# Dense stage of a three-stage transformer block: gates worked out behind the first weight split, norms of four tiles inside the last unit, odd residuals added on VectorE

## The reference, cut to what matters

```
x = rmsnorm(src + sa, norm1_w);  flat = x.reshape(S, C)
shared = swiglu(flat @ W_shared_in) @ W_shared_out
g_probs = softmax(flat @ Wg_gate + group_bias);  g_idx = argmax(g_probs)
e_probs = softmax(where(in_group, flat @ We_gate + expert_bias, -inf))
p_expert = e_probs * g_prob;  topv, topi = top_k(p_expert, 2);  w = scatter of topv
h = swiglu(flat @ W1_shared);  routed = sum over 8 experts of (h @ W2_experts[e]) * w[:, e]
out = rmsnorm(x + shared + routed, norm2_w)          # and the caller adds: x2 + out
```

## Time and profile before

| | |
|---|---|
| runs shown | 3588.77 us median of 3 (3583.67 to 3590.61) |
| profiled execution | 3591.36 us |
| its span, first to last instruction | 3589.5 us |
| TensorE busy | 3316.7 us, 92% of the span |
| VectorE / ScalarE / GpSimd busy | 1851.6 / 1485.4 / 1631.7 us |
| mean granted TensorE clock | 0.964 of full speed |

### The profile page before, as it was taken

The page is one execution under the profiler, slowest core; times in us unless marked ns, Lnnn a source line. Parts: engine busy times, 40 slices in busy tenths (PEclk is TensorE's granted clock), DMA queues, the critical chain, the costliest instruction groups (busy, mean ns, idle before and its releaser), DMA issues. The chain is left out here.

```text
span 3589.5 us, 52832 instructions
## 1 busy us (share of the span) xinstructions
PE 3316.7 (92%) x19140; PEld 2847.9 (79%) x19140; DVE 1851.6 (52%) x3010; ACT 1485.4 (41%) x2749; POOL 1631.7 (45%) x1122
## 2 busy tenths in 40 slices
PE   5999999999999999999999988899999586799995
PEld 4888888888888888888888876777777465578995
DVE  4454555555455555555545557566566537432213
ACT  3455555555555555555555541244344214221000
POOL 4354555555455555545545543143144035146663
PEclk9999999999999999999999989899999798899998
DMA  5211111111111011111111004100000300123220
GB/s 194 76 33 36 45 45 44 35 35 46 36 45 46 24 45 46 43 38 45 33 36 45 27 15 139 55 1 26 3 1 1 108 16 1 49 74 118 83 83 24
DMA packets 116510, 170.33 MB, mean 47 GB/s; under 512 B 12288, under 2 KB 89472, under 8 KB 107520
## 3 DMA queue, kind: packets, MB, share of 16 engines
q1 hardware_dynamic: 113408, 158.23, 14.0%
q0 software_dynamic: 2816, 8.46, 0.7%
HBM read 143.52 MB, written 23.13 MB: 46 GB/s over the span
## 5 line engine op out<-in xcount | busy, mean ns | idle before, releaser
L427 POOL TENSOR_TENSOR es<-es,e 128x512 f32<-128x512 f32 x480 | 622.7, 1297 | 966.7 <-ACT e L493 966.5
L489 ACT ACTIVATE e_hl<-sc 128x512 fp32r<-128x512 f32 x512 | 325.2, 635 | 739.1 <-DVE sc L557 738.8
L585 PE MATMUL ps_p<-c_hi,wkv_lo 128*128 128x512 f32 x1024 | 402.4, 393 | 4.5 <-PEq L115 4.5
L515 DVE TENSOR_TENSOR k_lo<-ps_p,k_hi 128x512 fp32r<-128x512 f32 x256 | 175.9, 687 | 438.9 <-ACT k_hi L455 438.9
L585 PE MATMUL ps_p<-c_lo,wkv_hi 128*128 128x512 f32 x1024 | 401.9, 393 | 0.0
L585 PE MATMUL ps_p<-wkv_lo,c_hi 128*128 128x512 f32 x1024 | 401.6, 392 | 0.0
L585 PE MATMUL ps_p<-wkv_hi,c_lo 128*128 128x512 f32 x1024 | 401.5, 392 | 0.0
L585 PE MATMUL ps_p<-c_hi,wkv_hi 128*128 128x512 f32 x1024 | 398.8, 389 | 0.0
L515 DVE TENSOR_TENSOR v_hl<-ps_p,v_hl 128x512 fp32r<-128x512 f32 x256 | 177.2, 692 | 428.8 <-ACT v_hl L455 427.9
L585 PE MATMUL ps_p<-wkv_hi,c_hi 128*128 128x512 f32 x1024 | 398.3, 389 | 0.0
L557 DVE TENSOR_SCALAR sc<-ps_s,topi 128x512 f32<-128x512 f32 x512 | 380.0, 742 | 0.3 <-PE ps_s L635 0.2
(11 more groups left out here) (399 smaller groups left out, 7136.4 us busy)
## 6 DMA issues: line engine op xcount, KB each, us to landing
raw<-in_ctx_t SPq DMA_DIRECT2D x64, 1024.0 KB, 4.9
dense_raw<-in_L_ffn_W_experts SPq DMA_DIRECT2D x64, 256.0 KB, 3.0
raw<-in_L_xattn_Wkv SPq DMA_DIRECT2D x4, 1024.0 KB, 5.0
q_hi_scratch<-qa_qh SPq DMA_DIRECT2D x16, 256.0 KB, 2.5
q_lo_scratch<-qa_ql SPq DMA_DIRECT2D x16, 256.0 KB, 3.4
q_hi<-q_hi_scratch SPq DMA_DIRECT2D x32, 128.0 KB, 5.1
q_lo<-q_lo_scratch SPq DMA_DIRECT2D x32, 128.0 KB, 4.7
o_t_scratch<-o_sb SPq DMA_DIRECT2D x32, 128.0 KB, 2.3
```

The costliest lines, as they stand in the source:

```text
L427: g.tensor_tensor(ES[:, GL], ES[:, GL], e, ALU.add).then_inc(summed, 1)
L489: a.activation(E2[:, s % 2, :, 0, :], sc, ACT.Exp, scale=DH ** -0.5).then_inc(exp_hi, 1)
L515: v.tensor_tensor(kv_slice(False, kind, n), ps_view(u, kind), kv_slice(True, kind, n).bitcast(F32), ALU.subtract).then_inc(p_free, 1)
L585: mm = t.matmul(ps_p[:, par % 2, :], lhs, rhs, start=m == 0, stop=m == 3 * KC - 1)
```

## The change

Three edits, all in or around the dense stage.

1. `route` moves from the end of stage_ffn_attend into stage_dense, behind VectorE's four splits of the first weights and ahead of its first multiplication. LG now lives outside both stages, in place of SEL, and SEL, which the dense stage now allocates itself, takes LG's part as a buffer of that stage. The comparison that sets SEL signals `chosen`, for which `rank` on TensorE waits. The exponential stands on ScalarE behind its four weight casts and ahead of the first silu. The scratch tiles RK and G lie in HS instead of PT, and the constant EARLIER comes as 16 more columns of ORDER instead of by a transfer of its own in the stage before. The instructions of `route` are the same.
2. In the last unit, VectorE takes the moments of tiles 0 to 3 and then finishes them (`finish(0)`: the small instructions, the scaling) right after the addition of slot B, ahead of the additions of slots 4 to 7. Each of tiles 4 to 7 has its moments taken right after its own last addition. Then comes `finish(1)`.
3. In `finish`, VectorE adds the residual of the odd tiles itself, after scaling; GpSimd adds that of the even ones. GpSimd still writes all eight tiles, in order.

```diff
 stage_ffn_attend, at its end on VectorE:
             v.wait_ge(logits_read, 1)
-            route(v, link)
 and on ScalarE:
-            a.wait_ge(g_shifted, 1)
-            a.activation(G[:, 14:20, :], G[:, 4:10, :], ACT.Exp).then_inc(g_expd, 1)

 stage_dense, GpSimd:
             for j in range(B):
-                g.wait_ge(scaled, j + 1)
-                g.tensor_tensor(OUT[:, j], ROWS[:, j], X2[:, j], ALU.add).then_inc(final, 1)
-                g.wait_ge(final, j + 1)
+                if j % 2:
+                    g.wait_ge(odd_final, j // 2 + 1)
+                else:
+                    g.wait_ge(scaled, j + 1)
+                    g.tensor_tensor(OUT[:, j], ROWS[:, j], X2[:, j], ALU.add).then_inc(final, 1)
+                    g.wait_ge(final, j // 2 + 1)
                 g.indirect_dma_start(out.rearrange("b p f -> (b p) f"), ...

 stage_dense, ScalarE:
                 a.copy(W_hi[:, A_, q], RAW[:, q]).then_inc(w_hi_done, 1)
+            a.wait_ge(g_shifted, 1)
+            a.activation(G[:, 14:20, :], G[:, 4:10, :], ACT.Exp).then_inc(g_expd, 1)
             branch(0)

 stage_dense, VectorE:
             v.wait_ge(order_in, 16)
+            route()
             v.tensor_copy(META[:, :, E_ALL], TOKEN).then_inc(meta_set, 1)
...
+            def moments_of(j):
+                moments(v, c, mom[:, j], ROWS[:, j], stats[:], rs[:, 3, 0:1])
+
+            def finish(hb):
+                s_ = slice(hb * H_, (hb + 1) * H_)
+                link(v.tensor_tensor(rs[:, 0], mom[:, s_, 0], mom[:, s_, 0], ALU.mult))
+                link(v.tensor_tensor(rs[:, 0], rs[:, 0], mom[:, s_, 1], ALU.add))
+                link(v.tensor_scalar(rs[:, 0], rs[:, 0], RMS_EPS, None, ALU.add))
+                rsqrt_cols(v, c, rs[:, 1], rs[:, 0], rs[:, 2])
+                for j in range(hb * H_, (hb + 1) * H_):
+                    v.scalar_tensor_tensor(out=ROWS[:, j], in0=ROWS[:, j], scalar=rs[:, 1, j % H_:j % H_ + 1], in1=N2[:], op0=ALU.mult, op1=ALU.mult
+                                           ).then_inc(scaled, 1)
+                    if j % 2:
+                        v.wait_ge(x2_in, 16 * B)
+                        v.wait_ge(scaled, j + 1)
+                        v.tensor_tensor(ROWS[:, j], ROWS[:, j], X2[:, j], ALU.add).then_inc(odd_final, 1)
             for u, (p, o) in enumerate(UNITS):
+                last = u == len(UNITS) - 1
...
+                    if last and j >= H_:
+                        v.wait_ge(added, B + m + 1)
+                        for jj in (range(H_) if j == B else (j,)):
+                            moments_of(jj)
+                    if last and j == B:
+                        finish(0)
+            finish(1)
-            v.wait_ge(added, B + NS * len(UNITS))
-            for hb in range(2):
-                ... the moments, the small instructions and the scaling of four tiles, twice

 stage_dense, TensorE, in rank():
+                t_.wait_ge(chosen, 1)
                 t_.matmul(bank(4)[:, 0:B], BEFORE, SEL[:, 0, :], start=True, stop=False, skip_group_check=True)

 program, outside both stages:
-        SEL = sb("sel", [P, 1, B])
+        LG = sb("lg", [P, GROUPS_E + E_ALL, B])
```

More of the change, by code:

```diff
@@ L1417, in _ @@
             sp.dma_start(WV[:], wv).then_inc(wkv_in, 16)
-            pieces = ((I[:], ident), (ROPE_T[:], rope_t), (EARLIER[:], earlier.partition_broadcast(P)),
+            pieces = ((I[:], ident), (ROPE_T[:], rope_t),
                       (BIAS[:, 0:GROUPS_E], g_bias.partition_broadcast(P)), (BIAS[:, GROUPS_E:], e_bias.partition_broadcast(P)),
@@ L1718, in hidden_piece, with stage_dense @@
     return [(dst[:, s], rows[:, :, s * HID + j * P:s * HID + (j + 1) * P]) for s in range(2)]
[L1721 removed]
+def stage_dense(nc, x2_d, xs_d, bs_d, ms_d, wts, order, norm2, ROWS, XT_hi, XT_lo, META, LG, RAW, out):
     w_in, w_out, w1, w2 = wts
@@ L1743, in stage_dense @@
         ONES = sb("ones", [P, P])
-        ORDER = sb("order", [P, 2 * P + B + B + 1])
+        ORDER = sb("order", [P, 2 * P + B + B + 1 + EPG * EPG])
         BEFORE, TOKEN, EDGE, I = (ORDER[:, a:b] for a, b in ((0, P), (P, P + B), (P + B, P + 2 * B + 1), (P + 2 * B + 1, 2 * P + 2 * B + 1)))
+        EARLIER = ORDER[:, 2 * P + 2 * B + 1:].rearrange("p (i j) -> p i j", i=EPG)
+        SEL = sb("sel", [P, 1, B])
+        RK = flat(HS[:])[:, 0:2 * EPG * EPG * B].rearrange("p (a i j b) -> p a i j b", a=2, i=EPG, j=EPG)
+        G = flat(HS[:])[:, 2 * EPG * EPG * B:][:, 0:30 * B].rearrange("p (n b) -> p n b", b=B)
         N0 = sb("n0", [P, 1])
@@ L2111, in _, with program @@
             g.sem_clear(range(nums[0], nums[-1] + 1))
-def program(nc, x, ctx_t, mask, ident, rope, causal, rope_t, earlier, order, wq, wkv, front, attend, w_proj, ffn, dense, norm2, out):
+def program(nc, x, ctx_t, mask, ident, rope, causal, rope_t, order, wq, wkv, front, attend, w_proj, ffn, dense, norm2, out):
     scratch = lambda n, s: nc.dram_tensor(n, s, F32, kind="Internal").ap()
@@ L2152, in program @@
         first_pieces = [piece for q in range(GP) for piece in hidden_piece(dense[0], DENSE_RAW, q, q)]
-        stage_ffn_attend(nc, ffn, (ident, rope_t, earlier), ROWS, XT_hi, XT_lo, META, SEL, first_pieces)
-        stage_dense(nc, x2, xs, bs, ms, dense, order, norm2, ROWS, XT_hi, XT_lo, META, SEL, DENSE_RAW, out)
+        stage_ffn_attend(nc, ffn, (ident, rope_t), ROWS, XT_hi, XT_lo, LG, first_pieces)
+        stage_dense(nc, x2, xs, bs, ms, dense, order, norm2, ROWS, XT_hi, XT_lo, META, LG, DENSE_RAW, out)
 FRONT = ["L0_xattn_Wo", "L0_xattn_bo"] + ["L0_attn_" + n for n in ("w_cq", "g_qnorm", "w_ckv", "g_kvnorm", "w_krope", "w_gate")]
@@ L2175, in tables @@
     order = np.concatenate([np.triu(np.ones((P, P)), 1), np.arange(TOK).reshape(B, P).T,
-                            np.tile(np.arange(B + 1) * P, (P, 1)), np.eye(P)], 1)
-    return {"order": f(order), "ident": f(np.eye(P)), "rope": f(rope), "causal": f(causal), "rope_t": f(rope_t), "earlier": f(np.tril(np.ones((EPG, EPG)), -1))}
+                            np.tile(np.arange(B + 1) * P, (P, 1)), np.eye(P), np.tile(np.tril(np.ones((EPG, EPG)), -1).reshape(1, -1), (P, 1))], 1)
+    return {"order": f(order), "ident": f(np.eye(P)), "rope": f(rope), "causal": f(causal), "rope_t": f(rope_t)}
 def kernel(**inputs):
@@ L2196 @@
     out = nc.dram_tensor("out", (B, P, D), F32, kind="ExternalOutput").ap()
-    program(nc, *(ap[n] for n in ("x", "ctx_t", "mask", "ident", "rope", "causal", "rope_t", "earlier", "order", "L0_xattn_Wq", "L0_xattn_Wkv")),
+    program(nc, *(ap[n] for n in ("x", "ctx_t", "mask", "ident", "rope", "causal", "rope_t", "order", "L0_xattn_Wq", "L0_xattn_Wkv")),
             [ap[n] for n in FRONT], [ap[n] for n in ATTEND], ap["L0_attn_w_proj"], [ap[n] for n in FFN], [ap[n] for n in DENSE], ap["L0_ffn_norm2_w"], out)
```

60 lines of the change are left out of this document (40 added, 20 removed).

## The result

The changed kernel took 3572.19 us (median of 6 runs, 3564.33 to 3572.79) beside 3589.55 us for the kernel before (6 runs, 3583.67 to 3592.53). The ratio is 0.9949, 95% interval 0.9936 to 0.9962: 18.3 us of 3589.55, between 14 and 23. A second timing gave 0.9947 (0.9933 to 0.9960). The forecast was 3570.0 in 3563 to 3578, a gain of 18.8 us.

A forecast was written before the change was run, and what follows sets the result against it. The prediction took a chain of waits through the dense stage and tail as the bound, mostly TensorE's; 6.1 + 12.7 = 18.8 us off 3591.36 gave 3572.6, and 2.6 less for the median 3570.0, range 3563 to 3578.

The forecast's parts named there:

- Part 1, route: At the dense stage's border: route's 6.07 us get covered, 4.2 us to spare at the third chunk; 6.1 us gained.
- The clock: TensorE's clock at the border: no difference taken, with bounds of 1.4 us less and 2.8 us more.
- Rival (c): At the border TensorE's clock does not fall: 1.4 us more gained, 3568.6; chance 0.08.
- Part 2, norms: In the last unit: four tiles' norms without TensorE noticing; together with the odd residuals 12.7 us gained.
- rival (b): Cover fails at the border (6.1 us lost) or in the last unit (4.1 lost): 3574 to 3576; chance 0.08.
- Part 3 and the exclusion: Tail: odd residuals on VectorE; its two-SBUF-input instructions and GpSimd's additions exclude each other; with the norms 12.7 us gained.
- (a): In the tail GpSimd's writes wait for VectorE's instructions: 2.3 us lost, 3572.3; chance 0.10.
- (d): Stages from 2137 us to the border, buffers moved 288 bytes, run slower; 2.0% undoes the gain; chance 0.03.
- (e): The border does not follow route's end, another engine arriving no earlier: only the tail's gain, 3576.1; chance 0.02.

The follow-up runs named there:

- route_longer_50: The changed kernel with 50 idle instructions, 10.0 us in all, behind route; 23.17 us from LG to the third chunk, not timed.
- border_matmuls: The changed kernel with nine unused products at the head of the dense stage; ratio to the kernel before 0.9939.
- best: second_half_dve with eleven unused TensorE products around the border; 3567.6 us, ratio to the kernel before 0.9931.
- last_unit_waits: The changed kernel, with the last unit's products for tiles 5 to 7 waiting for the addition right before; 42.99 us from slot B to last write, not timed.
- second_half_dve: The changed kernel with VectorE also adding the residuals of tiles 4 and 6, GpSimd only writing in the second half; ratio to the kernel before 0.9942.
- shift_only: The kernel before with SEL ten times as wide, so that buffers lie 288 bytes further on; ratio to the kernel before 0.9993.
- route_only: The kernel before with only route moved into the dense stage, the tail as before; ratio to the kernel before 0.9983.
- norms_only: The kernel before with only the first four tiles' norms moved into the last unit, GpSimd adding all residuals; ratio to the kernel before 0.9964.

## Why the prediction was right

**The sum.** 18.8 us forecast, 18.3 timed (14 to 23), 18.9 in the profiles. The forecast of 3570.0 lies 2.2 us under the median, which is within what the runs of one kernel spread. That 18.8 and 18.9 agree to 0.1 us is luck: the border gave 1.2 us less than forecast, the tail 0.4 more, and 0.9 us of the spans' difference come from stretches that were forecast to stay.

**Part 1, route.** Right as a mechanism in each step: the first cast 0.51 us behind LG, TensorE's idle time at the border 9.22 to 3.15 us, one table load behind the exponential, the first multiplication late (3106.68, 12.3 us behind LG's end; before it stood 16.2 behind, of which 6.07 were route, so it would have come after 10.1 with nothing in its way) and no wait at the third chunk. The slack left was 5.6 us where I had 4.2, because the third chunk itself came later. The term is mis-sized by 1.2 us: 6.1 forecast, 4.9 measured. TensorE's first product came 2.87 us behind LG's end, as forecast; the whole difference lies behind it, and is the clock.

**The clock.** The prediction took no difference between bounds of 1.4 us gained and 2.8 lost; 1.2 were lost. The six kernels with route moved and nothing more on TensorE, route_longer_50 with its wait left out, have 18.59 to 18.68 us, so this is no scatter. The upper bound took the low clock to last the ten us that it had lasted before; it lasted some 6.9, of which TensorE worked 5.6 instead of 3.05. What sets this length no run here shows. The reason I gave for the lower bound, that the clock might not fall in a pause of 3.15 us, was the weak part: in border_matmuls it fell without such a pause. Rival (c) was wrong for the kernel as it is, and became true in best, where filling the stretch ahead of the border as well took the whole cost of the slow products away, 18.59 - 16.11 = 2.5 us.

**Part 2, norms.** Right: no wait of TensorE in the last unit, and last_unit_waits shows what the cover is worth: without it 11.3 us come back. That is more than the 4.1 of rival (b), which left out that the clock falls in so long a wait and let the products follow each other without a handover.

**Part 3 and the exclusion.** The tail gave 13.1 us where 12.7 were forecast. The order of events came as worked out: from the first scaling of the second half to the last write 9.2 us forecast (3562.1 to 3571.3), 9.06 measured; the addition of tile 1 held up by GpSimd's (1.60 us), that of tile 3 not (0.69). Taken apart, part 2 gave most, 10.4 us alone, and part 3 3.8 alone or 2.7 behind part 2.

**The rivals.** (a) is refuted by second_half_dve; (b) by the changed trace, and both its covers were measured; (c) by the granted clock at the border; (d) by shift_only's timing; (e) by route_only. What made the first write of the tail wait 1.2 us is not settled: it waits 1.19 to 1.52 us in every trace here, whatever VectorE does, and costs nothing in the new order, since GpSimd rests afterwards.

## What to carry to other kernels

These are drawn from this one kernel. Small work on one engine between two stages costs its full length when the others stand idle (moving it gave 4.9 of 6.07 us here, and more slow products took the rest), and nothing when it is placed behind that engine's share of the next stage's start, as long as the slack there covers it; look for the first instruction that needs it there and count the slack. Work at the end of a loop can move in front of the last few steps if the producer is as many buffers ahead as there are steps left. And when two engines take turns in a tail, give the second engine's elementwise work to the first one if it is the second's queue that ends last. A gain at a stage's border should be read with the granted clock beside it: a shorter pause did not mean fewer products at the low clock.

## What the runs showed of the hardware that I had not expected

TensorE's granted clock went to 1.2 GHz although it had been working for about a microsecond again, after a stretch of ten-column transposes and two waits of 0.7 to 0.8 us (border_matmuls); with three products in and around those gaps, and eight behind them, it stayed at 2.4 GHz (best). What decides between the two is not shown. The fall and return at this border hardly differ between kernels with the same work around it: with route moved and nothing added on TensorE the first thirteen products start at the wide spacing, with route in its old place the first seven.

VectorE's instructions with two SBUF inputs and GpSimd's additions excluded each other down to tiny sizes: in the kernel before, the 128x4 instruction at 3566.31 took 1.00 us instead of 0.16, until GpSimd's addition of 3566.01 to 3567.28 had ended. The additions with one input in PSUM, the moments' instructions, and one-input small instructions beside a write were not held: L2022 took 0.48 at 3548.05 in the changed kernel while GpSimd added from 3547.48 to 3548.76.

Two cases don't fit this and stay open. L78, with one input, took 1.88 us in the kernel before, and in norms_only 0.17 beside a write. It and the 128x4 instruction of norms_only (1.72 us) have the same pattern: each began beside a write, 0.58 and 0.42 us ahead of GpSimd's next addition, and ended within 0.03 us of that addition's end.
